# Final weighted sums of a two-layer graph and expert network: one token tile in four computed by GpSimd

## The reference, cut to what matters

```python
    y_pairs = jnp.where(valid, y[flat_e, jnp.minimum(pos, CAP - 1)], 0.0)
    routed = (y_pairs.reshape(-1, K, d) * top_scores[..., None].astype(xf.dtype)).sum(axis=1)
    shared = jax.nn.silu(xf @ sw1) * (xf @ sw3) @ sw2
    return (shared + routed).reshape(bs, slen, d)
...
x = x + _L1_ffn_ref(_layernorm(x, axis=-1), ...)
```

## Time and profile before

| | us |
|---|---|
| median of 3 runs (lowest, highest) | 2105.18 (2103.22, 2107.63) |
| the profiled execution, its own time | 2106.05 |
| its span, first to last instruction | 2104.2 |
| DVE busy over the span | 1509.8 (72%) |
| POOL busy over the span | 1070.3 (51%) |
| PE busy over the span | 1910.8 (91%) |
| first and last start of the final sums (line 2303) | 2039.0 and 2100.7 |

### The profile page before, as it was taken

How to read it: one execution, slowest core, us unless ns; L and a number is a source line. 1 busy time by engine, 2 the same in 40 slices (tenths; PEclk the granted TensorE clock), 3 DMA queues, 4 the chain that set the end, 5 groups by cost and what they waited for, 6 DMA issues and landing times. The chain is left out here.

```text
span 2104.2 us, 38489 instructions
## 1 busy us (share of the span) xinstructions
PE 1910.8 (91%) x12194; PEld 1439.0 (68%) x12194; DVE 1509.8 (72%) x3332; ACT 1247.3 (59%) x1870; POOL 1070.3 (51%) x1266
## 2 busy tenths in 40 slices
PE   7999999992999999996689999999896899999996
PEld 6899888882888888886244454444443588878854
DVE  5777778753666666665589899889987477766659
ACT  4444444431666666665588878877775277767630
POOL 3355565533333333332655766767742377777740
PEclk9999999995999999999799999999998899999998
DMA  7444544214455555554424222123220255555559
GB/s 305 152 176 178 181 179 153 81 41 148 150 179 190 171 170 182 176 180 135 168 70 137 86 95 93 65 94 125 95 84 4 90 187 186 178 173 180 188 210 360
DMA packets 138148, 315.42 MB, mean 150 GB/s; under 512 B 36990, under 2 KB 67808, under 8 KB 133952
## 3 DMA queue, kind: packets, MB, share of 16 engines
q1 hardware_dynamic: 106560, 271.77, 38.4%
q0 software_dynamic: 31488, 42.39, 5.8%
HBM read 206.67 MB, written 151.56 MB: 170 GB/s over the span
## 5 line engine op out<-in xcount | busy, mean ns | idle before, releaser
L1906 DVE TENSOR_TENSOR c_att<-c_p_s,adj 128x1024 f32<-128x1024 f32 x256 | 300.3, 1214 | 55.5 <-PE c_p_s L1409 55.5
L1701 ACT ACTIVATE c_att<-c_att 128x1024 f32<-128x1024 f32 x256 | 268.7, 1056 | 117.6 <-DVE c_att L1906 110.7
L995 POOL DMA_INDIRECT moe_y<-b_y,b_goal x144 | 156.1, 1084 | 328.1 <-DVE b_y L1047 294.2
L2228 POOL DMA_INDIRECT moe_y<-d_y,d_goal x256 | 259.9, 1015 | 114.2 <-issue 54.4
L154 PE MATMUL b_p_y<-b_w2h,b_hh 128*128 128x256 f32 x576 | 169.4, 294 | 8.8 <-DVE b_hl L160 3.9
L476 POOL DMA_INDIRECT moe_in<-a_xn,a_rows x128 | 141.5, 1106 | 57.5 <-issue 28.9
L160 DVE TENSOR_TENSOR b_hl<-b_ht,b_hh 128x512 fp32r<-128x512 f32 (+1 forms) x160 | 101.6, 639 | 88.3 <-ACT b_ht L1153 88.3
L155 PE MATMUL b_p_y<-b_w2l,b_hh 128*128 128x256 f32 x576 | 160.8, 279 | 0.0
L156 PE MATMUL b_p_y<-b_w2h,b_hl 128*128 128x256 f32 x576 | 160.8, 279 | 0.0
L1365 POOL DMA_INDIRECT moe_in<-c_xn,c_rows x128 | 131.1, 1025 | 53.1 <-issue 37.8
L1422 PE MATMUL c_p_o<-c_att,c_xp 128*32 128x512 f32 x1024 | 139.0, 615 | 6.1 <-ACT c_att L1701 3.7
(11 more groups left out here) (273 smaller groups left out, 5736.3 us busy)
## 6 DMA issues: line engine op xcount, KB each, us to landing
b_w<-in_moe_w SPq DMA_DIRECT2D x80, 512.0 KB, 4.2
moe_in<-b_zeros SPq DMA_DIRECT2D x65, 520.0 KB, 11.0
d_xin<-moe_in SPq DMA_DIRECT2D x64, 520.0 KB, 3.6
adj<-in_adj SPq DMA_DIRECT2D x32, 1024.0 KB, 5.6
b_xin<-moe_in SPq DMA_DIRECT2D x32, 520.0 KB, 5.7
c_g<-moe_y SPq DMA_DIRECT2D x32, 512.0 KB, 6.1
moe_y<-c_zeros SPq DMA_DIRECT2D x32, 512.0 KB
d_w<-in_moe_w SPq DMA_DIRECT2D x64, 256.0 KB
```

Source lines behind the costliest of these rows:

```text
L995: pool.indirect_dma_start(out=m["moe0_y"], out_offset=bass.IndirectOffsetOnAxis(ap=goal[:, h, t:t + 1], axis=0), in_=y[:, h, t, :], in_off ...
L1701: act.activation(part, part, ACT.Tanh).then_inc(att_ready, 1)
L1906: dve.tensor_tensor(att[:, u % 2, 2 * c:2 * c + 2, :], p_s[:, 2 * c:2 * c + 2, :], adj[:, h, u % T, :].unsqueeze(1).broadcast_to([P, 2, N] ...
L2228: pool.indirect_dma_start(out=m["moe1_y"], out_offset=bass.IndirectOffsetOnAxis(ap=goal[:, h, t:t + 1], axis=0), in_=y[:, h, t, :], in_off ...
```

## The change

In the final sums the tiles t = 0, 1, 2 of a graph stay with DVE (six instructions in place of eight), and the tile t = 3 goes to POOL. [...] It waits for its own second multiplication before the first addition, and for the first addition before the second. SP waits for both engines before it stores the graph's x and loads into the buffer again. In the attention phase the semaphore `cd_split` is given up, and the two steps that it counted are counted in `init`, whose number stood at 4 before them; they wait for the same instructions as before.

```diff
-        cd_split = sem("cd_split")
+        CDH_SPLIT, CDL_SPLIT = 5, 6
...
-                pe.wait_ge(cd_split, 2)
+                pe.wait_ge(init, CDL_SPLIT)
...
-            act.activation(cdh[:], cd[:], ACT.Copy).then_inc(cd_split, 1)
+            act.activation(cdh[:], cd[:], ACT.Copy).then_inc(init, 1)
...
-            dve.wait_ge(cd_split, 1)
-            low_part(dve, cdl[:], cd[:], cdh[:]).then_inc(cd_split, 1)
+            dve.wait_ge(init, CDH_SPLIT)
+            low_part(dve, cdl[:], cd[:], cdh[:]).then_inc(init, 1)
...
-        step, stored = sem("step"), sem("stored")
+        step, pool_step, stored = sem("step"), sem("pool_step"), sem("stored")
+        DVE_TILES = T - 1
...
-                sp.wait_ge(step, 2 * T * (n + 1))
+                sp.wait_ge(step, 2 * DVE_TILES * (n + 1))
+                sp.wait_ge(pool_step, 3 * (n + 1))
...
+            def sum_last_tile(n):
+                b = ORDER[n]
+                g0, g1 = (ring[n % DEEP][:, k * T + T - 1, :] for k in range(2))
+                at = b * 2 * T + T - 1
+                tile = x[:, b * T + T - 1, :]
+                pool.wait_ge(s_sum[n % DEEP], 32 * (n // DEEP + 1))
+                own_wait(pool, mark_pool)
+                if b in LATER:
+                    pool.wait_ge(lx4_ready, TB * (DONE + b - OWN) + TB)
+                    own_wait(pool, mark_pool)
+                pool.tensor_scalar(g0, g0, m["gate1"][:, at:at + 1], None, ALU.mult)
+                pool.tensor_scalar(g1, g1, m["gate1"][:, at + T:at + T + 1], None, ALU.mult).then_inc(pool_step, 1)
+                pool.wait_ge(pool_step, 3 * n + 1)
+                own_wait(pool, mark_pool)
+                pool.tensor_tensor(tile, tile, g0, ALU.add).then_inc(pool_step, 1)
+                pool.wait_ge(pool_step, 3 * n + 2)
+                own_wait(pool, mark_pool)
+                pool.tensor_tensor(tile, tile, g1, ALU.add).then_inc(pool_step, 1)
+            for n in range(B):
+                sum_last_tile(n)
...
-                    for t in range(T):
+                    for t in range(DVE_TILES):
                         at = b * 2 * T + k * T + t
                         if k == 1:
-                            dve.wait_ge(step, 2 * T * n + t + 1)
+                            dve.wait_ge(step, 2 * DVE_TILES * n + t + 1)
```

## The result

Over 22 runs of each kernel the changed one took 2109.16 us (median) against 2105.2 before. The ratio is 1.0018 with a 95% interval of 1.001 to 1.0025: slower by 3.8 us, with 2.1 to 5.3 inside the interval. One run of each lies far off, at 10480 and 4884 us; the ratio is of the others. The profiled execution has a span of 2109.5 us, 5.3 more than that of before.

The account below looks back on a forecast made before the run. DVE (3.89 us per graph) and transfers (3.82) were both taken as near full. DVE's 2101.2 less 12.7 plus 16.9 contention gave 2105.4, plus 0.8 for buffers 2106.2: +5.0 us, 2110.2, range 2102.5 to 2115.5.

Parts of the forecast that it names:

- 12.7 us off DVE: Final sums: 32 of DVE's 128 sums go, at 0.396 us each, 12.7 us of its work.
- Worth 4.2 us at the most: Final sums: transfers at 3.82 us per graph cap the gain at 4.2 us, even if POOL's part were free.
- POOL alone, 3.60 us per graph: Final sums: POOL's two multiplications, two additions and waits take 3.60 us per graph undisturbed, 57.6 for 16.
- Alone it would fit: Final sums: without contention POOL would end at 2093.4, or by the loads at 2097.3.
- rival 1: Final sums: transfers hide everything and contention is small; -3.9 us, 2101.3; chance 0.14.
- Side by side: Final sums: DVE loses 0.49 us per POOL addition, 0.19 per multiplication; POOL takes 4.24 us per graph.
- factor of 0.83: Final sums: share of DVE's time in instructions with two SBUF inputs, scaling its contention delay to 16.9 us.
- Waits for loads: Final sums: transfers bound no more; buffers coming free only after the later engine add 0.8 us.
- rival 4: Final sums: the ring starves, POOL holds buffers longest and loads are issued late; +7 to +9, 2113; chance 0.15.
- The signs I named: Profile after, final sums: longer sums and POOL instructions, DMA share under 1.00, no DVE idle time, loads not ending the chain.
- rival 3: Final sums: whole instructions exclude each other, 5.7 us per graph; +29, 2134; chance 0.04 including all above.
- the two engines take turns, one instruction each: Read from four normalizations beside four bias additions: 0.75 us apart, where one alone is 0.38 long.

Follow-up runs that it names:

- POOL idle: Changed kernel with POOL's work in the final sums removed and the fourth tile left unsummed: ratio 0.9979 to the kernel before, 4.4 us less.
- POOL writing only: Changed kernel with POOL's four instructions per graph made memsets on free buffers, waits kept, fourth tile unsummed: ratio 0.9991 to the kernel before, 1.9 us less.

## Why the prediction was right, and where it wasn't

**The number.** Forecast +5.0 us, measured +3.8 (2.1 to 5.3); the last sum in the trace ended at 2106.4, forecast 2106.2. That the two agree so closely is in part luck. Two terms were off, in opposite directions: DVE's delay by the meetings (16.9 us forecast, 11.4 measured) and the waits for loads (0.8 and 6.2). The trace's stage also began 1.3 us earlier than that of before; measured from the first load, the stage grew by 6.6 us and not by 5.0. And DVE was forecast to end last (2105.4, POOL 2103.0); it ended at 2104.85, and POOL last, at 2106.43. Of POOL's 13.0 us of waits for loads 6.4 stand between its graphs, where the forecast had none.

**12.7 us off DVE: right.** **"Worth 4.2 us at the most": right for this kernel.** POOL idle gave 4.4, and the load of graph 15 landed at 2094.8, forecast 2093.7. It is a cap for three buffers, which keep the transfers waiting until the first store: with five 9.0 came.

**POOL alone, 3.60 us per graph: right.** The first graph, undisturbed, runs from 2034.60 to 2038.27. "Alone it would fit" was too cheap: I had 0.3 us for it (the cap of 4.2 against the 3.9 of rival 1), and POOL writing only, about as long, cost 2.5 over POOL idle by the ratios and 1.0 by the stages, because it holds the buffers longer.

**Side by side: mechanism right, one factor too large.** Prices taken from other stages: 0.49 us for a sum that meets an addition, measured 0.41 to 0.47 (0.36 in the kernel whose last graph DVE does alone); 0.19 for a multiplication, measured 0.17 to 0.22. The factor of 0.83, DVE's share of time in sums, was meant to say how many meet. For multiplications it did (29 of 32). For additions 14 of 32 cost DVE something, 0.44. DVE's delay was 11.4 us (66 sums late by 0.137 and 30 by 0.078 in the mean) and not 16.9. Such a share holds only if the two engines run at random against each other. In the changed kernel both start a graph together when its rows land, POOL's additions come 2.3 us later (2094.05 to 2096.33 in one graph), when DVE's six sums are nearly over, and DVE's next instruction is often a shared-expert one or a wait.

Who loses when an addition meets a sum goes by who starts first, as single instructions of the changed kernel show. Of the 16 first additions 10 began 0.04 to 0.06 us behind a sum and took 1.00 to 1.02 us instead of 0.73. Of the 16 second additions 12 began 0.03 to 0.42 us ahead of a sum, and the sum was late, by 0.51 us where it began right behind and by 0.12 where it began 0.42 behind. So first additions have a mean of 909 ns and second ones of 743, and 12 of the 14 sums that lost to an addition lost to a second one.

**Waits for loads: the term that failed.** I argued that at over 4.1 us per graph transfers (3.82) bound no more, and added 0.8 for the ring; DVE waited 6.2 us for loads. The pace of transfers did not bind, their latency did. With three buffers each goes through 6.0 us of landing (median, up to 8.9), some 4.2 of POOL, and about 0.9 of SP's issues: 11.1 to 14.0 us for three graphs, 3.7 to 4.7 each. This was rival 4's mechanism, to which I gave 0.15; it took part in the outcome beside the contention. Five buffers took the waits away and 4 us with them.

**The signs I named.** The DMA share of 2060 to 2080 under 1.00: 0.92. Multiplications over 0.97: 1.02 to 1.10. POOL's additions over 0.85: the first of each graph 0.89 and 0.96, the second 0.74, so 0.83 over all, a little under. Sums at 0.60 to 0.70: 0.596. "DVE without idle time": wrong, for the reason above, and "several us of idle time" of DVE was named as a sign that the forecast is wrong. DVE had 6.2 us of it: the time is inside the range, but this half of the mechanism was not. "A load no longer ends the chain": POOL's last tile ends it, but loads hold 31% of it.

**Whole-instruction exclusion (rival 3): out.** It would have made multiplications the dearer ones; by themselves they cost 2.5 us and additions 8.8. Single instructions say the same, and they also contradict "the two engines take turns, one instruction each": a multiplication ran from 2053.62 to 2054.66, and a sum beside it from 2053.79 to 2054.49. That POOL's memsets left the sums at 478 ns agrees with the Trainium skill, "SBUF — State Buffer", section "Who interferes with whom", which has a GpSimd instruction that only writes not contend with a Vector instruction of two SBUF inputs.

**What stays open.** Why so many first additions begin just 0.04 us behind a sum was not tried. The 8.2 us between POOL idle and the changed kernel split into 2.5 and 5.7 by ratios whose intervals are some 2 us wide on either side; that the reads matter is carried by the lengths of the sums (478 or 596 ns), the size of the split is not known well. No kernel here beats the one before beyond its interval with all sums made. A way to it that was not tried would be five buffers (9.0 us are there) with the fourth tile's work on something that doesn't read beside DVE.

## What to carry to other kernels

Before giving POOL a part of DVE's elementwise work, look in the trace for places where the two already run together, and compare the lengths of single instructions by where the inputs lie; here that gave each price within about a quarter. Then ask how often they will meet, from the order in which both start, not from shares of busy time. And where a ring of buffers is shared, the later engine sets when a buffer comes free: count latency plus holding time over the number of buffers, even when the transfers' rate has room.

## What was not expected of the hardware

- POOL's multiplication by a per-partition number, 0.92 us long, costs a simultaneous two-input sum of DVE 0.17 to 0.22 us; its addition, 0.73 us long, costs 0.41 to 0.47. The shorter instruction costs more than twice as much.
- Moving the multiplications to ACT made DVE's sums longer (622 ns against 596), because nearly every addition (30 of 32, from 14) then made a sum late.
- The kernel before took 2105 to 2107 us in three of the comparisons and 2197 on the chip of the fourth. There the stage of the second experts begins at the same time as elsewhere (1658 to 1662 us), and the first load of the final sums goes out at 2111 to 2124 instead of 2027 to 2032; the final sums themselves are no longer (73.8 us with five buffers). The whole difference lies between those two points; its cause is not known.
